# Expert feed-forward over 39 blocks of 256 slots of one expert, weights stationary

## What is computed

```python
xn = _layernorm(x, axis=-1)
x = x + _L0_attn_ref(xn, W1, b1, Wp, bp) + _L0_ffn_ref(xn, gate_w, expert_gate, expert_up, expert_down, shared_gate, shared_up, shared_down)

def _ffn(x, gw, uw, dw):                       # gw, uw: 352 x 128, dw: 128 x 352
    return jax.nn.silu(x @ gw.T) * (x @ uw.T) @ dw.T
shared = _ffn(xf, shared_gate, shared_up, shared_down)
probs = jax.nn.softmax(xf @ gate_w.T, axis=-1)             # 8 experts
topw, topi = jax.lax.top_k(probs, 2)                       # 2 experts for each token
topw = topw / (topw.sum(-1, keepdims=True) + 1e-20)
comb = zeros.at[arange(T)[:, None], topi].add(topw)
routed = sum over experts e of _ffn(xf, gate_e, up_e, down_e) * comb[:, e]
return shared + routed
```

## Time and profile before

| | us |
|---|---|
| runs of the kernel before | 562.12, 555.89, 562.30 |
| their median | 562.12 |
| the profiled execution, its own time | 559.99 |
| its span in the trace | 558.3 |

### The profile page before, as it was taken

How to read it: one execution, slowest core, us unless ns; L and a number is a source line. 1 busy time by engine, 2 the same in 40 slices (tenths; PEclk the granted TensorE clock), 3 DMA queues, 4 the chain that set the end, 5 groups by cost and what they waited for, 6 DMA issues and landing times.

```text
span 558.3 us, 13933 instructions
## 1 busy us (share of the span) xinstructions
PE 513.5 (92%) x4584; PEld 332.5 (60%) x4585; DVE 398.1 (71%) x753; ACT 310.4 (56%) x684; POOL 324.7 (58%) x382
## 2 busy tenths in 40 slices
PE   8888999889998998899989889999999999999995
PEld 3334444444444444343443348999999999977673
DVE  7886668887878777877887675565555555548896
ACT  2016777777767767777776753333333333365542
POOL 5439742342466777767777744667666444575442
PEclk9875999999979989999997989999999999999998
DMA  5416631040211245522211112211221222434554
GB/s 166 157 46 197 211 143 65 21 154 3 77 60 44 94 170 196 176 71 90 78 54 36 49 34 65 68 57 57 73 59 57 62 70 57 119 108 130 155 153 147
DMA packets 52156, 53.46 MB, mean 96 GB/s; under 512 B 5744, under 2 KB 39568, under 8 KB 51856
## 3 DMA queue, kind: packets, MB, share of 16 engines
q1 hardware_dynamic: 47616, 43.71, 24.7%
q0 software_dynamic: 4352, 8.95, 4.8%
q10 hardware_dynamic: 144, 0.20, 0.1%
HBM read 20.38 MB, written 17.90 MB: 69 GB/s over the span
## 4 chain that ended last, share of the span: by engine, by line
PE 66%; DVE 12%; ACT 7%; issue 6%; DMA 4%; POOL 3%; DVEq 1%; SPq 0%; ACTq 0%; POOLq 0%
PE av_bank L879 13%; PE mx_pair L824 9%; PE av_bank L1053 9%; PE st_banks L852 5%; DVE neg_max L1543 4%; PE st_banks L1064 4%; DVE o_sb L1719 3%; ACT probs L1244 3%; PE av_bank L902 2%; PE st_banks L759 2%; PE mx_pair L1039 2%; DMA out<-o_sb 2%; PE mx_pair L1043 2%; PE mx_pair L1044 2%; PE mx_pair L1042 2%
## 5 line engine op out<-in xcount | busy, mean ns | idle before, releaser
L1543 DVE TENSOR_REDUCE neg_max<-mx_pair 128x2 f32<-128x256 f32 (+3 forms) x256 | 203.7, 822 | 63.4 <-PE mx_pair L835 61.0
L1244 ACT ACTIVATE probs<-st_banks 128x512 f32<-128x512 f32 (+1 forms) x384 | 181.0, 524 | 63.7 <-PE st_banks L852 62.0
L705 POOL DMA_INDIRECT y_tok<-y_sb,y_rows x72 | 70.0, 972 | 74.1 <-ACT y_sb L1349 59.6
L852 PE MATMUL st_banks<-q_st,k_st 32*128 32x128 f32 (+3 forms) x512 | 96.3, 407 | 13.4 <-ACT probs L1244 7.7
L824 PEld LDWEIGHTS mx_pair<-k_st,q_st 31*128 31x128 f32 x512 | 43.4, 190 | 101.8 <-issue 62.7
L879 PE MATMUL av_bank<-probs,v_wide 128*18 128x384 f32 (+3 forms) x1024 | 98.9, 461 | 3.5 <-ACT av_sb L1257 2.6
L824 PE MATMUL mx_pair<-k_st,q_st 31*128 31x256 f32 (+3 forms) x512 | 90.1, 395 | 11.3 <-DVE neg_max L1543 11.1
L629 POOL DMA_INDIRECT sorted_x<-xn_rows,slot_idx x64 | 63.8, 997 | 13.3 <-issue 12.7
L1342 ACT ACTIVATE sg<-mx_pair 128x352 f32<-128x352 f32 x72 | 33.4, 463 | 62.3 <-PE mx_pair L1044 62.3
L852 PEld LDWEIGHTS st_banks<-q_st,k_st 32*128 32x128 f32 x512 | 48.2, 191 | 27.5 <-ACT probs L1244 18.6
L588 POOL TENSOR_SCALAR_AFFINE_SELECT probs<-probs 128x1024 f32<-128x1024 f32 x32 | 35.0, 1094 | 45.8 <-ACT probs L1244 45.7
(11 more groups left out here) (214 smaller groups left out, 895.9 us busy)
## 6 DMA issues: line engine op xcount, KB each, us to landing
sorted_x<-zeros SPq DMA_DIRECT2D x8, 580.5 KB, 4.1
xg<-sorted_x SPq DMA_DIRECT2D x36, 129.0 KB, 2.2
picked<-y_tok SPq DMA_DIRECT2D x16, 256.0 KB, 3.7
q_st<-q_hi SPq DMA_DIRECT2D x14, 256.0 KB, 2.5
k_st<-k_hi SPq DMA_DIRECT2D x14, 256.0 KB, 2.5
egu_lo<-in_e_gu SPq DMA_DIRECT2D x2, 1408.0 KB, 6.6
x_all<-in_x SPq DMA_DIRECT2D x8, 256.0 KB, 3.6
att_T<-a_T SPq DMA_DIRECT2D x8, 256.0 KB, 2.1
```

What stands on the lines that cost most here:

```text
L705: pool.indirect_dma_start(y_tok, bass.IndirectOffsetOnAxis(ap=y_rows[:, t, k:k + 1], axis=0), y_sb[t % 2][:, k, :], None).then_inc(y_st[t ...
L852: ins = pe.matmul(st_banks[:, i % 3, lo:lo + w], k_st[buf][32 * j:32 * j + 32, g, kb * P:(kb + 1) * P], q_st[buf][32 * j:32 * j + 32, g, k ...
L1244: act.activation(dst, src, ACT.Exp, scale=SCALE).then_inc(st_free, 1)
L1543: ins = dve.tensor_reduce(neg_max[:, g, h:h + 2, qb], mx_pair[i % 2][:, :, lo:lo + (qb + 1) * P], AX.X, ALU.max, negate=True)
```

## The change

- The rows of an expert are rounded up to 256, and `sorted_x` is cut into `NBLK` = 39 blocks of 256 slots, 9984 in all. A block belongs to one expert. `past`, `columns` and `block_start` shrink from 72 to 39 entries. The zero fill has 13 pieces instead of 8, two at each of s = 0 to 5 and one at s = 6.
- `gate_up` has the weights as the stationary side: three chunks of features (128, 128, 96), for each gate and up, three matmuls whose moving side is the 256 tokens. So 18 fp32r matmuls of 256 columns, at fixed addresses. The result has features on the partitions already, so `hid_transposes` and `hiddenT_out` are gone, and DVE's product writes `hidT`.
- The weights are split for each block: ACT copies the 704 columns of the block's expert to `w_hi` (`weights_high`), DVE subtracts to get `w_lo` (`weights_low`). Each of the two reads the expert's column into a register of its own queue. The 16 splits at the end of attention are gone. The first two `weights_high` are on ACT's queue at the end of s = 28 and s = 29.
- The banks are used by parity: gate and up products in banks 0, 1, 2 for even blocks and 3, 6, 5 for odd ones. TensorE's order for block t is `x_step(t+1)`, `down(t-2)`, `gate_up(t)`. The down product thus comes two blocks later.
- TensorE reads one register for each block (`down_column`) instead of four.
- At the start, `x_step(0)` and `x_step(1)` come first, then `gate_up(0)`, the first transposes, `x_step(2)`, `gate_up(1)` (its third chunk waits for `a_last`), and then the transposes back.
- GpSimd's 12 splits come at every third block. `down` of the last block comes after the first chunk of `shared_up`.

The core of the diff:

```diff
-NTILE = 2 * T // P + NX
-SLOTS = NTILE * P
+BLK = 2 * P
+NBLK = 2 * T // BLK + NX - 1
+SLOTS = NBLK * BLK
-FILLS = 8
+FILLS = 13
...
             def gate_up(t, par):
                 n = at(t, par)
+                pe.wait_ge(xg_split, held(pe, n + 1))
+                pe.wait_ge(w_split, held(pe, n + 1))
+                if not (isinstance(n, int) and n < 2):
+                    pe.wait_ge(hid_done, held(pe, FC * (n - 1) + PRIME_HID))
+                x_hi, x_lo = (w[par][:].rearrange("p k m -> p (k m)") for w in (xgT_hi, xgT_lo))
+                for c in range(FC):
+                    m = min(P, F - c * P)
+                    if isinstance(n, int) and n == 1 and c == FC - 1:
+                        pe.wait_ge(a_last, 1)
+                    for a in range(2):
+                        dst, cols = expert_bank(par, c)[0:m, a * BLK:(a + 1) * BLK], slice(c * P, c * P + m)
+                        pe.matmul(dst, w_hi[par][:, a, cols], x_hi, start=True, stop=False)
+                        pe.matmul(dst, w_hi[par][:, a, cols], x_lo, start=False, stop=False)
+                        ins = pe.matmul(dst, w_lo[par][:, a, cols], x_hi, start=False, stop=True)
+                    ins.then_inc(gu_done, 1)
...
+            def expert_block(t, par):
+                n = at(t, par)
+                col = down_column(n)
+                x_step(*shift(t, par, 1))
+                down(*shift(t, par, -2), col)
+                gate_up(t, par)
...
+            def weights_high(t, par):
+                n = at(t, par)
+                col = block_column(n, 0, mybir.EngineType.Activation, (NX - 1) * 2 * F)
+                act.activation(w_hi[par][:].rearrange("p a f -> p (a f)"), egu[:].rearrange("p x a f -> p (x a f)")[:, bass.ds(col, 2 * F)],
+                               ACT.Copy).then_inc(w_high, 1)
...
-            with act.Fori(1, NPAIR // 2 - 1) as i:
+            with act.Fori(1, NBLK // 2 - 1) as i:
                 for par in range(2):
-                    expert_step(("r", i), par, True, True, True)
+                    sigmoid_part(("r", i), par)
+                    x_out(("r", i + 1), par)
+                    weights_high(("r", i + 1), par)
+                    result(*shift(("r", i), par, -1))
...
+            def weights_low(t, par):
+                n = at(t, par)
+                col = block_column(n, 0, mybir.EngineType.DVE, (NX - 1) * 2 * F)
+                dve.wait_ge(w_high, n + 1)
+                dve.tensor_tensor(w_lo[par][:].rearrange("p a f -> p (a f)"), egu[:].rearrange("p x a f -> p (x a f)")[:, bass.ds(col, 2 * F)],
+                                  w_hi[par][:].bitcast(F32).rearrange("p a f -> p (a f)"), ALU.subtract).then_inc(w_split, 1)
...
-            for x in range(4):
-                split_weights(x)
             turned(GROUPS - 1)
-            for x in range(4, NX):
-                split_weights(x)
...
+            def hidden(t, par):
+                n = at(t, par)
+                if not (isinstance(n, int) and n < 2):
+                    dve.wait_ge(y_done, n - 1)
+                for c in range(FC):
+                    m = min(P, F - c * P)
+                    dve.wait_ge(sg_done, FC * n + c + 1)
+                    dve.tensor_tensor(hidT[par][0:m, c, :], sg[0:m, c, :], expert_bank(par, c)[0:m, BLK:2 * BLK], ALU.mult).then_inc(hid_done, 1)
...
+            with dve.Fori(1, NBLK // 2 - 1) as i:
                 for par in range(2):
-                    expert_step(("r", i), par, True)
+                    hidden(("r", i), par)
+                    x_low(("r", i + 1), par)
+                    result_rows(("r", i + 1), par)
+                    weights_low(("r", i + 1), par)
```

More of the change, by code:

```diff
@@ L341, in res_bank_of, with expert_bank, shared_banks, block_column @@
         def res_bank_of(b):
-            return bank[0] if isinstance(b, int) and b == B - 1 else bank[6]
+            return bank[4] if isinstance(b, int) and b == B - 1 else bank[6]
+        def expert_bank(par, c):
+            return bank[((0, 1, 2), (3, 6, 5))[par][c]]
+        def shared_banks(c):
+            return [(bank[4], bank[5]), (bank[0], bank[1]), (bank[2], bank[3])][c]
+        def block_column(n, k, engine, most):
+            clamped = "DVE clamps the expert before it multiplies"
+            _, cols = nc.values_load_multi_w_load_instructions(
+                columns[0:1, bass.ds(n, 1), k:k + 1].rearrange("o s c -> o (s c)"), engines=[engine], min_val=0,
+                max_val=most, skip_runtime_bounds_check_because=clamped)
+            return cols[0]
         def held(engine, value):
@@ L698, in _ @@
                 (sdn_hi[0:FR, 2], sdn_lo[0:FR, 2], sdn[0:FR, 2])]
-            every = NPAIR // (len(splits) + 1)
-            for t in range(NPAIR):
+            every = NBLK // (len(splits) + 1)
+            for t in range(NBLK):
                 pool.wait_ge(y_rows_kept, t + 1)
@@ L1049, in down @@
+            def down(t, par, col):
+                n = at(t, par)
+                pe.wait_ge(hid_done, held(pe, FC * (n + 1) + PRIME_HID))
+                pe.wait_ge(y_out, held(pe, n + PRIME_Y))
                 w = edn[:].rearrange("p x c e -> p (x c e)")
@@ L1326, in _ @@
                     bias_out()
-            g_bank, xgT_bank, y_bank = bank[0:2], bank[4], bank[7]
+                if s == GROUPS - 4:
+                    act.wait_ge(columns_set, 2)
+                    for i in range(2):
+                        act.wait_ge(egu_ld[i], 16)
+                    weights_high(0, 0)
+                if s == GROUPS - 3:
+                    weights_high(1, 1)
+            xgT_bank, y_bank = bank[4], bank[7]
             def x_out(t, par):
@@ L1660, in _ @@
+            for i in range(2):
+                dve.wait_ge(egu_ld[i], 16)
+            dve.wait_ge(columns_set, 2)
+            for t in range(2):
+                weights_low(t, t)
+            for t in range(2):
+                x_low(t, t)
+                result_rows(t, t)
+            hidden(0, 0)
             dve.wait_ge(t_last, 1)
             normalise(GROUPS - 1, bank[5]).then_inc(a_last, 1)
[L1663 to L1672 removed]
@@ L1690, in _ @@
-            for t in range(2):
-                expert_step(t, t, True)
-            with dve.Fori(1, NPAIR // 2 - 1) as i:
-                for par in range(2):
-                    expert_step(("r", i), par, True)
-            for t in range(NPAIR - 2, NPAIR):
-                expert_step(t, t % 2, t + 1 < NPAIR)
+            x_low(2, 0)
+            result_rows(2, 0)
+            weights_low(2, 0)
+            hidden(1, 1)
+            x_low(3, 1)
+            result_rows(3, 1)
+            weights_low(3, 1)
@@ new lines, in _ @@
+            with dve.Fori(1, NBLK // 2 - 1) as i:
+                for par in range(2):
+                    hidden(("r", i), par)
+                    x_low(("r", i + 1), par)
+                    result_rows(("r", i + 1), par)
+                    weights_low(("r", i + 1), par)
+            for t in range(NBLK - 3, NBLK):
+                hidden(t, t % 2)
+                if t + 2 < NBLK:
+                    x_low(t + 2, t % 2)
+                    result_rows(t + 2, t % 2)
+                    weights_low(t + 2, t % 2)
```

263 lines of the change are left out of this document (101 added, 162 removed).

## The result

| | runs | median, us | ratio to the kernel before, 95% interval |
|---|---|---|---|
| before | 4 | 561.87 | |
| after | 4 | 547.27 | 0.9753 [0.9713, 0.9794] |

The kernel is faster by 14.6 us. The profiled execution has a span of 545.2 us, against 558.3 before: 13.1 us less. I had forecast 3.9 less, and a range that began at 548.5. Some executions of each kernel fall into a slower state: the medians in this document are over all executions, the ratios over the others.

What follows compares the result with a forecast made beforehand. TensorE's instructions were taken to bound the expert stage. Way in -2.9, stage -2.0 and attention +1.0 sum to -3.9 us, giving 556.1 from the profiled execution or 558.2 from the median; predicted 557.0, range 548.5 to 567.

Steps and rivals of the forecast that it cites:

- the stage: Expert stage on TensorE: 142.3 us after against 144.3 before, so -2.0 us, at 3.86 us a block.
- attention: Two weights_high copies on ACT ahead of exponentials, 0.8 to 1.2 us each: +1.0 us taken, range 0 to 2.4.
- the way in: From attention's end to gate_up(2): it starts at 338.6 us instead of 341.5, so -2.9 us.
- The bound: Expert stage lasts as long as TensorE's instructions take one after another, 4.26 us a pair before.
- The price of a matmul: Gate and up in the expert stage: 0.117 us per 256-column fp32r matmul, 18 a block, 2.11 us.
- The change-over: Switch to the next fp32r matmul: about 0.08 us, staying in each block and moving behind down.
- The bubble: Every second pair's longer down (1.48 for 1.34 us) and x transposes (0.09 us longer); the forecast kept the means.
- the bubbles go too: Rival, expert stage: alternation vanishes and matmuls take 0.112 us; 3.66 us a block, about 549 us in all; chance 0.15.
- DVE as the bound: Rival, expert stage: weights_low subtraction at 1.65 us makes DVE need 4.1 us a block; 565 to 567 us; chance 0.16.
- Weight loads: Taken as hidden under 256-column matmuls; the rival has them exposed, 67 us over forecast, some 623 us; chance 0.04.
- a slack of about 2.5 us: Expert stage: ACT and DVE need some 3 us for weights of block t+2, leaving about 2.5 us to spare.

Runs made afterwards that it cites:

- e18_pad: Kernel after with each block's two x transposes done twice, chip 15: 555.15 us, ratio to before 0.9936, mean block 3.84 us (unedited beside it 547.45 us, 3.65).
- e2_noread: Kernel before with the four registers read once ahead of the stage, chip 10: 565.83 us, ratio 0.9951, mean pair 4.147 us.
- e3_nowait: Kernel before, hidden transposes reading a constant and the wait for the product moved ahead of gate_up, chip 10: 569.43 us, ratio 1.0043, mean pair 4.269 us.
- e5_late_w: Kernel after with the first two weights_high moved to the end of attention, chip 10: 579.77 us, ratio to before 1.0035.
- e10_tail2: Kernel after with the last down behind two shared_up chunks, as in the kernel before, chip 10: 574.66 us, ratio to before 1.0004.
- e13_nosplit: Kernel after with GpSimd's splits moved from between the blocks to block 35, chip 3: 598.11 us, ratio to before 1.0502, mean block 4.16 us.

## Why the prediction was wrong

The sum was -3.9, the two traces give -13.1. Of the 9.2 between them, the stage is 7.8, attention 1.0, the tail 1.3, and the way in has the other sign, 0.9.

- **The bound: right.** TensorE's instructions one after another set the stage, before and after. `e18_pad` shows it directly.
- **The price of a matmul: right.** 0.117 for full chunks, 0.114 for the 96-wide ones.
- **The change-over: 0.08 that no row has. This is the first step that failed.** I took 0.08 of the 0.66 of the hidden transposes for a change-over to fp32r, and added it to gate and up. But in the earlier trace rows the two x transposes take 0.22 and the twelve instructions of down 1.34, so 0.11 each, and six transposes at 0.11 are 0.66 with nothing left. After is the same: the first fp32r matmul behind down takes 0.12, like those that follow. With 0.02 for the narrow chunks the 18 matmuls take 2.09 for 2.19, -3.7 over 37 blocks.
- **The bubble: carried over. The second failed step, and the larger.** I took the mean of the two kinds of pair for down (1.41) and for the x transposes (0.265), though my own rival named TensorE's late queue as a cause. Measured 1.34 and 0.22, -4.3 over 37 blocks. `e2_noread` against `e3_nowait` shows that in the kernel before the bubble needs the register read, and not the late wait. Why it is gone in after, which still has a load a block, is open: the shorter queue (16 instructions for 26) is my reading. The two steps together make -0.21 a block, -7.8.
- **The rival "the bubbles go too" was the true case.** It forecast 3.66 a block and 549; measured 3.65 and 547.3. I gave it 0.15, because I held its other half, 0.112 a matmul, against it. The two halves were independent: the bubble went, the spacing stayed 0.117. That its sum came out right was luck in part: the spacing was too low and the change-over of 0.08 too high, and the two cancelled (2.10 for 2.09). A rival that joins two claims should be split before it gets a chance.
- **The way in: -2.0 for -2.9.** I had `gate_up(0)` at 330.1, without issue in front; there are still 0.70 us of issue and it starts at 330.61, as before (330.67). And 1.01 us of issue stand in front of the loop's first x step, where I took 0.43 from the kernel before. Add 0.3 for a longer x step and down; what lies between went 0.5 faster than I had put it.
- **Attention: 0 for +1.0.** One of the two copies (0.78) and a register read of 0.45 are on the chain, yet the end of attention is the same within 0.2. I can't say what gave it back. `e5_late_w` doesn't tell, since its ratio can't resolve 1 us and its way in is longer.
- **The tail: -1.3, not forecast.** The last down comes after one shared chunk, not two; the last row of `y_tok` lands 8.6 us after the shared stage begins, for 10.0. That this is the cause was only read from the traces: `e10_tail2` (1.0004) could not resolve it.
- **DVE as the bound: no, by a wide margin.** The subtraction takes 0.92, and even twice of it costs nothing measurable.
- **Weight loads: hidden**, at 0.117 with loads of 128 rows each. The Trainium skill, page "TensorE: Matmul & The Clock Gate", section "Part 3: Packing small matmuls — row/col tiling", says in one place that a load overlaps running matmuls only when it goes to another row group, which would have them exposed. This trace contradicts that, as the earlier trace rows did. The same section also has a load pulled ahead when it targets the background weight buffer; the hidden loads agree with that, though no trace here shows which buffer a load goes to.
- **What no step foresaw:** that on another chip the same change brings nothing, or 0.6% in one group of runs. The forecast had a slack of about 2.5 us for the weights and 1.5 for the result, and asked only what DVE and ACT would do with it. TensorE's increments on chips 10 and 3, up to 2.5 us late, use it all.

## What to carry to other kernels

Read a stream's bill from one row to the next, and divide each row by its count before taking a change-over out of it. When a stall alternates with a period of two, find what causes it before taking its mean into the forecast: here TensorE's own queue was late in the pair with the loop's branch, 0.12 us a pair in the mean, and without its register load the alternation was gone. Look in the trace whether an added instruction ran: two edits here added reads that nothing used, and both traces are the unedited kernel's. And when a change shortens a stage to which other engines hand back, measure it on more than one chip: hand-offs with 1.5 us to spare were enough on two chips and not on two others.

## What the runs showed of the hardware

- One program, four chips: ratio to the kernel before 0.975 and 0.980 on two, 0.994, 1.003 and 1.005 on the third (three groups of runs), 1.001 and 1.000 on the fourth, at a granted clock of 0.99 to 1.00 in the stage each time.
- On chips 10 and 3 TensorE's semaphore increments came up to 2.5 us after the recorded (modelled) end of the matmul, with a median of 0.43 us in the expert stage of the kernel after and 0.014 us in that of `e3_nowait`; on the other two chips 0.014 us. Those of DVE and ACT had a median of 0.01 us.
- A stage can run evenly for eight blocks and then fall into a slower rhythm (4.08 and 4.5 by turns in `e13_nosplit`) that it doesn't leave.
- fp32r matmuls cost by moving columns almost alone: 0.117 us at 256, 0.161 at 352, 0.233 at 512, with 0.114 at 256 where the stationary side has 96 columns. A change to them from fp32 work costs nothing that shows.
- A register load takes 0.28 us of ACT's sequencer, 0.30 to 0.33 of TensorE's. It was on the chain where ACT's queue had just run dry (0.45 us in attention), and nowhere in the even blocks of the first chip.
